# A Gram-matrix product in three passes on split parts, with one part kept in HBM between batches

## The chip, the cores and the metric

One core of a Trainium2 chip runs the whole kernel. The metric is the device time of one execution in microseconds (us). The profile and the trace come from one further execution of the same program; their times are in us from the start of its span, and durations of single instructions are in ns where it says so.

## What is computed

A decoder layer in fp32 on 8 batches of 512 tokens with 512 features. Three blocks follow each other, each with a layer norm ahead of it and a residual behind it:

1. A linear attention without softmax. The reference writes it token by token:

```python
Q = jnp.einsum('btae,aeqf->qbtaf', x, qw)
pre = jnp.einsum('qbtaf,buqf->qbtau', Q, x)
attn = jnp.einsum('qbtau,buqg->abtqg', pre, x)
out = jnp.einsum('abtk,akg->btag', attn, combiners)
```

   Since nothing nonlinear stands between the factors, the kernel first forms the Gram matrix of the normalised tokens per head q, G_q = y_q^T y_q (128 x 128), then T_q = G_q times the combiners of that q (128 x 512), then M = the queries times T, and last x + rstd * (centred x) M. "Combiner product" is the product T_q.

2. Cross attention with a context of 512 tokens per batch, softmax, biases.

3. A shared expert of 704 hidden features plus a mixture of 16 experts with top-2 routing and a capacity per expert.

## The kernel before, in words

**Three passes.** Most large products are not done as plain fp32 matmuls. Each operand is split once into an upper part (a copy into the type fp32r, made by ScalarE) and a lower part (the difference of the value and its upper part, made by VectorE or GpSimd). `three_pass` (L62 to L72, its matmuls are all on L71) then adds three matmuls per product: upper times upper, upper times lower, lower times upper. The queries, scores, values, probabilities and all expert products go that way. The Gram matrix (L785, from the `f32_group` helper), the combiner product (L886), the product M (L785 too) and A (L921) are plain fp32 matmuls. A fp32 matmul shows as two records in the trace.

**Order of the work.** The order is written out by hand in `phase2` (`order`, a list of named steps), and every engine walks the same list and does its own share of each step. Iteration i mixes the cross attention of batch i with the linear attention of batch i+1: Y1T(i), V(i), ST0(i+1), LN0(i+1), MEAN(i+1), STORE(i-1), Q(i), G(i+1), T(i+1), SC(i), M(i+1), PT(i), C(i+1), A(i+1), LN1(i+1), PV(i), LN2(i). On TensorE, step G ends with the first of four score tiles of batch i (`scores(b - 1, 0)`, 12 matmuls), then T does four fp32 matmuls of 512 columns, then SC does the other three score tiles (36 matmuls), then M. At i = 0 the step V(0) has been done earlier. Names such as INIT, WV and QB occur for batch 0 alone.

**The steps that the change touches.** ScalarE's part of G copies the bank with the Gram matrix to the tile G (row 12 of the scratch area, where a row is 2 KB of every partition), and counts `s_ev["G"]`; TensorE's part of T waits for that count (`drained(pe, "G", b)`). ScalarE's part of T copies the four results to y. In SC, VectorE takes the maximum of each score tile (L701), and ScalarE writes the exponentials to `prob`, rows 88 to 91. These rows hold the raw query weights during INIT. The combiners (CT, 1 MB) lie in rows 4 to 7 from the start (L282) and are read by T alone. Row 43 holds zeros that two DMAs of GpSimd write to HBM early on (`fill_tables`, semaphore `s_pad`); nobody reads it later in phase 1 save the tokens of the experts near the end.

**The DMA queue of SyncE.** SyncE issues its DMAs in the order of the list: in step A the transposed x of the next batch after A's last matmul (L311, L312), in MEAN the store of 512 means (L302), a wait for its landing and the load of the row of means into all partitions (L306), in STORE the batch's output and normalised tokens (L325, L328) and the x of three batches ahead, in C the context of the next batch (L291). GpSimd subtracts the row of means from the transposed x (L379), and TensorE's step A waits for that.

**Behind the batches.** After the last batch come the experts (`phase2`, L71 with 512 or 320 columns and L1432), with weights streamed by SyncE, split by ScalarE (L1246) and GpSimd (L1188).

Of the kernel before, what the change touches and what calls it, by code (L numbers as in the profile page):

```python
# [29 lines left out]
F32 = mybir.dt.float32  # L30
F32R = mybir.dt.float32r
# [43 lines left out]
def build(nc, a):  # L75
    Y = nc.dram_tensor("tokens_normed", (N + PAD, 2 * D), U16, kind="Internal").ap()

    slots = nc.dram_tensor("slots", (E * CAP, 2), F32, kind="Internal").ap()
    means = nc.dram_tensor("means", (B, S), F32, kind="Internal").ap()
    with ExitStack() as ctx:  # L80
        def sb(name, shape, dt):
            return ctx.enter_context(nc.sbuf_tensor(name, shape, dt))

        base, _ = nc.bump_sbuf(ROWS * D * 4)
        placed = []

        def at(row, shape, dt=F32):

            placed.append(row)
            return nc.alloc_sbuf_tensor_at(f"buffer{len(placed)}", [P] + shape, dt, offset=base + int(row * D * 4))  # L90

        shared = {
            "ident": sb("ident", [P, P], F32),
            "slot_list": sb("slot_list", [P, NSLOT, 2], F32),
            "slots": slots,
            "means": means,
            "ps": [ctx.enter_context(nc.psum_tensor(f"ps{i}", [P, 512], F32)) for i in range(BANKS)],
        }
        attn = phase1(nc, ctx, a, Y, shared, at)
        phase2(nc, ctx, a, Y, shared, at, attn)  # L100


def phase1(nc, ctx, a, Y, shared, at):
    out = a["out"]
    ident, slot_list, slots = shared["ident"], shared["slot_list"], shared["slots"]
    means = shared["means"]
    ps = shared["ps"]

    def sb(name, shape, dt):
# [2 lines left out]
    def sem(name):  # L112
        return ctx.enter_context(nc.semaphore(name))
# [36 lines left out]
    VWH, VWL = at(30, [NC, D], F32R), at(34, [NC, D], F32R)  # L150
    QT = at(0, [H, H, P])
    CT = at(4, [H, H * P])
    key_row, bv_all = at(50, [D]), at(51, [D])
    rw = sb("rw", [P, NC, E], F32)
    rwp = sb("rwp", [P, NC, 2 * E], F32R)
# [16 lines left out]
    xT = at(8, [NC, S])  # L172
    mean_row, zeros = at(42, [S]), at(43, [D])
    G = at(12, [H * P])
    M = at(13, [H * P])
    y1h, y1l = at(68, [NC, S], F32R), at(72, [NC, S], F32R)
    qh, ql = at(52, [NC, S], F32R), at(56, [NC, S], F32R)
# [76 lines left out]
    s_mean, s_mstored, s_mrow = sem("s_mean"), sem("s_mstored"), sem("s_mrow")  # L254
    s_xT, s_centred = sem("s_xT"), sem("s_centred")
    s_cnt = sem("s_cnt")

    def sync(sp):
        def load_x(b):
            if b >= XS:  # L260

                sp.wait_ge(s_out, 16 * (b - XS + 1))
            sp.dma_start(x[b % XS][:], a["x"][b].rearrange("(t p) d -> p t d", p=P)).then_inc(s_x[b % XS], 16)

        def small_loads():
            for dst, src in ((bias_col[:, 0:NC], a["bq"].rearrange("(c p) -> p c", p=P)),
                             (bias_col[:, NC:2 * NC], a["bk"].rearrange("(c p) -> p c", p=P)),
                             (bv_all[:], a["bv"].partition_broadcast(P)),
                             (rb_all[:], a["rb"].partition_broadcast(P)),
                             (rw[:], a["rw"].rearrange("(c p) e -> p c e", p=P))):  # L270
                with nc.allow_non_contiguous_dma(reason="a few columns of biases"):
                    sp.dma_start(dst, src).then_inc(s_small, 16)  # L272

        for j in range(NC):
            rows = slice(j * P, (j + 1) * P)
            sp.dma_start(wq_raw[:, j, :], a["WqT"][rows, :]).then_inc(s_wqk[j], 16)
            sp.dma_start(wk_raw[:, j, :], a["WkT"][rows, :]).then_inc(s_wqk[j], 16)  # L277
            if j == 1:
                load_x(0)
        small_loads()  # L280
        sp.dma_start(wv_raw[:], a["Wv"].rearrange("(c p) n -> p c n", p=P)).then_inc(s_wv, 16)
        sp.dma_start(CT[:], a["CT"]).then_inc(s_w, 16)  # L282
        sp.dma_start(QT[:], a["QT"]).then_inc(s_w, 16)

        def load_transposed(b):
            sp.dma_start(xT[:], a["xT"][b].rearrange("(c p) n -> p c n", p=P)).then_inc(s_xT, 16)

        load_transposed(0)

        def load_context(b):  # L290
            sp.dma_start(craw[:], a["ctxT"][b].rearrange("(c p) k -> p c k", p=P)).then_inc(s_c, 16)  # L291

        load_context(0)

        def step(name, b):
            if name == "C" and b >= 1:
                sp.wait_ge(s_cl, NC * b)
                load_context(b)
            if name == "MEAN":
                sp.wait_ge(s_mean, b + 1)  # L300
                with nc.allow_non_contiguous_dma(reason="one number per partition and tile"):
                    sp.dma_start(means[b].rearrange("(t p) -> p t", p=P), mean[:]).then_inc(s_mstored, 16)  # L302
                sp.wait_ge(s_mstored, 16 * (b + 1))
                if b >= 1:
                    sp.wait_ge(s_centred, NC * b)
                sp.dma_start(mean_row[:], means[b].partition_broadcast(P)).then_inc(s_mrow, 16)  # L306
                if b == 0:
                    for first in range(1, XS):
                        load_x(first)
            if name == "A" and b + 1 < B:  # L310
                filled(sp, "A", b, NT - 1)  # L311
                load_transposed(b + 1)  # L312
            if name == "TURN":
                if b == 0:
                    sp.wait_ge(s_out, 16 * (B - 1))
                    for stored in s_yout:
                        sp.wait_ge(stored, 16 * NT * (B - 1) // 2)
                for t in range(NT):
                    sp.dma_start_transpose(turned(b, t)[:], Y[b * S + t * P:b * S + (t + 1) * P, :])\
                        .then_inc(s_turn, 16)  # L320
            if name == "STORE":
                rows = slice(b * S, (b + 1) * S)
                sp.wait_ge(s_base, NT * (b + 1))
                sp.wait_ge(s_out, 16 * b)
                sp.dma_start(out[rows, :].rearrange("(t p) d -> p t d", p=P), x[b % XS][:]).then_inc(s_out, 16)  # L325
                for t in range(NT):
                    sp.wait_ge(s_halves, NT * b + t + 1)
                    sp.dma_start(Y[b * S + t * P:b * S + (t + 1) * P, :],  # L328
                                 halves(b, t)[:].rearrange("p two d -> p (two d)")).then_inc(s_yout[t % 2], 16)
                if b + XS < B:  # L330
                    load_x(b + XS)
        return step
# [97 lines left out]
    def scalar(act):  # L430
# [15 lines left out]
        def step(name, b):  # L446
# [55 lines left out]
            if name == "Q":  # L502
                for c in range(NC):
                    filled(act, "Q", b, c)
                    bank = bank_of("Q", b, c)
                    act.activation(qh[:, c, :], bank[:], ACT.Identity, bias=qbias[:, 2 * c:2 * c + 1])\
                       .then_inc(s_qh, 1)
            if name == "G":
                filled(act, "G", b)
                bank = bank_of("G", b, 0)  # L510
                copy(G[:], bank[:]).then_inc(s_ev["G"], 1)
            if name == "SC":
                for t in range(NT):
                    act.wait_ge(s_nb, NT * b + t + 1)
                    filled(act, "SC", b, t)
                    bank = bank_of("SC", b, t)
                    act.activation(prob[:, t, :], bank[:], ACT.Exp, bias=nbias[:, t:t + 1],
                                         scale=SCALE, accum_out=rsum[:, t:t + 1]).then_inc(s_ev["SC"], 1)
# [21 lines left out]
    def vector(dve):  # L540
# [68 lines left out]
        def step(name, b):  # L609
# [71 lines left out]
            if name == "Y1T":  # L681
                for c in range(NC):
                    dve.wait_ge(s_y1h, NC * b + c + 1)
                    filled(dve, "Y1T", b, c)
                    bank = bank_of("Y1T", b, c)
                    dve.tensor_tensor(y1l[:, c, :], bank[:], y1h[:, c, :].bitcast(F32), ALU.subtract)\  # L686
                        .then_inc(s_ev["Y1T"], 1)
            if name == "Q":
                for c in range(NC):
                    dve.wait_ge(s_qh, NC * b + c + 1)  # L690
# [91 lines left out]
    def tensor(pe):  # L782
# [20 lines left out]
        def step(name, b):  # L803
# [74 lines left out]
            if name == "T":  # L878
# [3 lines left out]
                    drained(pe, "W", 0, NC - 1)  # L882
                drained(pe, "Q", b - 1, 3)
                drained(pe, "G", b)
                for q in range(H):
                    pe.matmul(bank_of("T", b, q)[:], G[:, q * P:(q + 1) * P], CT[:, q, :],  # L886
                              start=True, stop=True).then_inc(s_mm["T"], 1)
            if name == "SC":
                if b == B - 1:
                    drained(pe, "V", b, 1)  # L890
# [57 lines left out]
def phase2(nc, ctx, a, Y, shared, at, attn):  # L948
# [70 lines left out]
    for i in range(-1, B):  # L1019
# [13 lines left out]
            steps.append(("V", 0))  # L1033
        if i == 0:
            steps.remove(("V", 0))
        for name, b in steps:
            if 0 <= b < (1 if name in ("INIT", "WV", "QB") else B):
                order.append((name, b))
# [448 lines left out]
```

## Time and profile before

| | |
|---|---|
| median of 3 runs | 1865.12 us (1864.83 to 1865.19) |
| the profiled execution's own time | 1865.53 us |
| its span | 1863.8 us |
| TensorE busy | 1836.5 us, 99% of the span |
| TensorE weight loads | 1616.4 us, 87% |
| VectorE, ScalarE, GpSimd busy | 834.7, 745.2, 880.4 us |

The busy time of TensorE is a union of records whose ends are modelled, so that a record can reach over the start of the next. The distance from start to start, or a piece of the chain of work, tells what a matmul costs in the stream.

### The profile page before, as it was taken

Reading aid. Unit: us, or ns where it says so; the run is one execution under the profiler, and the core shown is the slowest. Engines: PE = TensorE matmul, PEld = TensorE weight load, DVE = VectorE, ACT = ScalarE, POOL = GpSimd, SP = SyncE. Lnnn points to the kernel's source line nnn. Section 1 sums busy time; section 2 is a strip of 40 time slices with the busy share of each in tenths; the row PEclk is TensorE's granted clock in tenths of the full one; section 3 lists DMA queues with packets and bytes.
Section 4 is the critical chain, followed back from the end, with each engine's and each line's share of the span. In section 5 each row is a group of like instructions: output and inputs, shape, how many; then the busy total and the mean of one; then the engine's idle time right before and its main releaser. Section 6 shows DMA issues by size and latency. Waiting matters only on the chain.

```text
span 1863.8 us, 27056 instructions
## 1 busy us (share of the span) xinstructions
PE 1836.5 (99%) x10096; PEld 1616.4 (87%) x10096; DVE 834.7 (45%) x2015; ACT 745.2 (40%) x1468; POOL 880.4 (47%) x759
## 2 busy tenths in 40 slices
PE   7899999999999999999999999999999999999997
PEld 4788888888887887888899999999999999999996
DVE  3565567556765444343342334433444334443332
ACT  2344443444454333332444344443444434444331
POOL 2235333533563423222656665566655666556631
PEclk9899999999999999999999999999999999999999
DMA  7303212322273333321766666666666676666722
GB/s 238 108 25 119 96 63 80 120 98 73 92 180 57 47 46 74 52 46 18 160 153 153 146 142 129 156 153 148 141 130 155 156 147 142 131 152 157 143 46 29
DMA packets 218098, 209.68 MB, mean 112 GB/s; under 512 B 137424, under 2 KB 137424, under 8 KB 217712
## 3 DMA queue, kind: packets, MB, share of 16 engines
q1 hardware_dynamic: 192672, 154.85, 31.3%
q0 software_dynamic: 25296, 53.11, 16.8%
q8 instruction: 80, 1.31, 0.3%
q14 instruction: 50, 0.41, 0.1%
HBM read 129.63 MB, written 48.92 MB: 96 GB/s over the span
## 4 chain that ended last, share of the span: by engine, by line
PE 97%; POOL 1%; SPq 1%; DMA 0%; DVE 0%; ACT 0%; issue 0%; DVEq 0%; ACTq 0%; POOLq 0%
PE ps L71 65%; PE ps L1432 23%; PE ps L785 4%; PE ps L921 2%; PE ps L886 2%; PE ps L791 1%; POOL buffer L379 0%; DMA buffer<-in_wts 0%; POOL buffer L387 0%; SPq L272 0%; DMA rw<-in_rw 0%; ACT buffer L437 0%; PE ps L866 0%; POOL buffer L1188 0%; SPq L277 0%
## 5 line engine op out<-in xcount | busy, mean ns | idle before, releaser
L71 PE MATMUL ps<-buffer,buffer 128*128 128x320 f32 (+1 forms) x6816 | 1227.2, 341 | 2.1 <-DVE buffer L686 2.1
L71 PEld LDWEIGHTS ps<-buffer,buffer 128*128 128x128 f32 x6816 | 1106.0, 188 | 107.9 <-issue 3.5
L1188 POOL TENSOR_TENSOR buffer<-buffer,buffer 128x512 fp32r<-128x512 f32 x289 | 380.0, 1481 | 249.7 <-ACT buffer L1246 249.4
L1432 PE MATMUL ps<-buffer,buffer 128*128 128x512 f32 x1904 | 437.5, 390 | 0.8 <-DVE buffer L1334 0.8
L1432 PEld LDWEIGHTS ps<-buffer,buffer 128*128 128x128 f32 x1904 | 355.7, 188 | 75.1 <-POOL buffer L1188 1.4
L1246 ACT ACTIVATE buffer<-buffer 128x512 fp32r<-128x512 f32 (+1 forms) x491 | 294.1, 651 | 164.9 <-PE ps L1432 93.8
L1288 ACT ACTIVATE buffer<-ps 128x320 f32<-128x320 f32 (+1 forms) x240 | 112.5, 469 | 599.1 <-PE ps L71 585.1
L1350 DVE TENSOR_TENSOR ps<-ps,buffer 128x320 f32<-128x320 f32 (+2 forms) x198 | 100.2, 506 | 489.0 <-ACT buffer L1288 468.0
L1235 POOL DMA_INDIRECT out_tokens<-buffer,slot_list x80 | 125.9, 1574 | 185.4 <-DVE buffer L1380 177.1
L424 POOL DMA_INDIRECT slots<-pairs,slot_u x64 | 63.5, 993 | 182.2 <-DVE slot_u L772 165.1
L432 ACT ACTIVATE buffer<-ps 128x512 fp32r<-128x512 f32 (+1 forms) x148 | 81.6, 600 | 120.1 <-PE ps L71 39.9
L437 ACT ACTIVATE buffer<-buffer,shift,rstd 128x512 f32<-128x512 f32 x96 | 70.4, 805 | 135.2 <-DVE shift L579 135.2
L1380 DVE TENSOR_SCALAR buffer<-ps,slot_list 128x512 f32<-128x512 f32 x80 | 59.7, 746 | 112.2 <-PE ps L1432 112.2
L1334 DVE TENSOR_TENSOR buffer<-ps,buffer 128x320 fp32r<-128x320 f32 (+2 forms) x198 | 96.5, 488 | 11.0 <-ACT buffer L1246 10.0
L1201 POOL DMA_INDIRECT buffer<-tokens_normed,slot_list x80 | 83.5, 1044 | 28.5 <-issue 28.5
L398 POOL TENSOR_TENSOR buffer<-buffer,buffer 128x512 f32<-128x512 f32 x32 | 42.1, 1348 | 116.0 <-DVE shift L579 105.2
L1246 ACT ACTIVATE buffer<-ps 128x320 fp32r<-128x320 f32 (+2 forms) x198 | 86.3, 436 | 0.3 <-DVE ps L1350 0.3
L387 POOL TENSOR_TENSOR buffer<-buffer,buffer 128x512 fp32r<-128x512 f32 x32 | 41.1, 1320 | 91.1 <-ACT buffer L432 91.1
L1318 DVE COPY buffer<-buffer 128x512 uint16<-128x512 uint16 x80 | 72.7, 931 | 0.5
L1350 DVE TENSOR_TENSOR buffer<-ps,buffer 128x512 f32<-128x512 f32 (+1 forms) x42 | 29.0, 690 | 96.7 <-ACT buffer L1288 96.2
L563 DVE BATCH_NORM_STATS2 stats<-buffer 128x6 f32<-128x512 f32 x96 | 61.2, 682 | 0.5
L701 DVE TENSOR_REDUCE smax<-ps 128x1 f32<-128x512 f32 x32 | 22.1, 691 | 86.4 <-PE ps L71 86.4
(116 smaller groups left out, 1116.6 us busy)
## 6 DMA issues: line engine op xcount, KB each, us to landing
buffer<-in_wts SPq DMA_DIRECT2D x289, 256.0 KB
buffer<-in_x SPq DMA_DIRECT2D x8, 1024.0 KB, 6.1
buffer<-in_xT SPq DMA_DIRECT2D x8, 1024.0 KB, 5.5
buffer<-in_ctxT SPq DMA_DIRECT2D x8, 1024.0 KB, 7.9
out_tokens<-buffer SPq DMA_DIRECT2D x8, 1024.0 KB, 6.0
tokens_normed<-buffer SPq DMA_DIRECT2D x32, 256.0 KB, 3.0
out_tokens<-buffer POOLq DMA_DIRECT2D x32, 256.0 KB, 5.4
buffer<-means SPq DMA_DIRECT2D x8, 256.0 KB, 4.6
```

What stands on the lines that cost most here:

```text
L71: last = pe.matmul(out, left, right, start=(c == 0 and i == 0), stop=(c == len(parts) - 1 and i == 2))
L432: return act.activation(dst, src, ACT.Copy)
L785: last = pe.matmul(out, left, right, start=(i == 0), stop=(i == len(pairs) - 1))
L1188: pool.tensor_tensor(wl[n % RING][:], wraw[n % RAW][:], wh[n % RING][:].bitcast(F32), ALU.subtract).then_inc(s_wl, 1)
L1201: pool.indirect_dma_start(xn[:, t, :], None, Y[:, :], rows_at(groups[g][1], t), bounds_check=N + PAD - 1).then_inc(s_xg, 16)
L1235: pool.indirect_dma_start(out[:, :], rows_at(part, t), ost[:, t, :], None, bounds_check=N + PAD - 1, compute_op=ALU.add).then_inc(s_add[t] ...
L1246: return act.activation(dst, src, ACT.Copy)
L1288: act.activation(silu[u % TMP][0:rows_of(c), 0:n], bank[0:rows_of(c), 0:n], ACT.Silu)\
L1318: dve.tensor_copy(halves_of(t)[:, :, :, 0], xp[t][:, NC:2 * NC, :]).then_inc(s_xlow, 1)
L1334: dve.tensor_tensor(lo[:, first:first + n], product_of(u)[0:rows, 0:n], hh[0:rows, c, first:first + n].bitcast(F32), ALU.subtract).then_in ...
L1350: dve.tensor_tensor(product_of(u)[0:rows_of(c), 0:n], up_bank[u % 2][rows, 0:n], silu[u % TMP][0:rows_of(c), 0:n], ALU.mult).then_inc(s_ht, 1)
L1432: ins = pe.matmul(down_bank[n % 2][:], left, right, start=(c == 0 and i == 0), stop=(c == FC - 1 and i == len(passes) - 1))
```

## The change

From batch 1 on the combiner product T is done with `three_pass` on split parts; batch 0 stays a plain fp32 product. The parts of the combiners are made once, in iteration 0: a new step SPLIT has ScalarE copy CT to `ct_hi` (rows 88 to 91, type fp32r) and SyncE store that to a new tensor `combiners` in HBM (1 MB); a new step LOW has VectorE write the difference over CT itself (`ct_lo`, rows 4 to 7). As the exponentials overwrite rows 88 to 91 in every batch, SyncE loads `ct_hi` again from HBM after step A of batches 1 to 6, for T of batches 2 to 7. In G, from batch 1 on, ScalarE writes `g_hi` (row 12) and VectorE then writes `g_lo` (row 43), and VectorE's instruction now counts `s_ev["G"]`. ScalarE's step SC of batch 0 waits for the store of `ct_hi`.

```diff
+    ct_hi, ct_lo = at(88, [H, H * P], F32R), at(4, [H, H * P], F32R)
+    g_hi, g_lo = at(12, [H * P], F32R), at(43, [H * P], F32R)
...
     # SyncE
             if name == "A" and b + 1 < B:
                 filled(sp, "A", b, NT - 1)
                 load_transposed(b + 1)
+                if b >= 1:
+                    sp.dma_start(ct_hi[:].bitcast(F32), combiners).then_inc(s_ct_loaded, 16)
+            if name == "SPLIT":
+                sp.wait_ge(s_ct_hi, H)
+                sp.dma_start(combiners, ct_hi[:].bitcast(F32)).then_inc(s_ct_stored, 16)
...
     # ScalarE
+            if name == "SPLIT":
+                for q in range(H):
+                    copy(ct_hi[:, q, :], CT[:, q, :]).then_inc(s_ct_hi, 1)
             if name == "G":
                 filled(act, "G", b)
                 bank = bank_of("G", b, 0)
-                copy(G[:], bank[:]).then_inc(s_ev["G"], 1)
+                if b == 0:
+                    copy(G[:], bank[:]).then_inc(s_ev["G"], 1)
+                else:
+                    copy(g_hi[:], bank[:]).then_inc(s_g_hi, 1)
             if name == "SC":
+                if b == 0:
+                    act.wait_ge(s_ct_stored, 16)
...
     # VectorE
+            if name == "LOW":
+                for q in range(H):
+                    dve.wait_ge(s_ct_hi, q + 1)
+                    dve.tensor_tensor(ct_lo[:, q, :], CT[:, q, :], ct_hi[:, q, :].bitcast(F32), ALU.subtract)\
+                        .then_inc(s_ct_lo, 1)
+            if name == "G" and b >= 1:
+                if b == 1:
+                    dve.wait_ge(s_pad, 32)
+                dve.wait_ge(s_g_hi, b)
+                filled(dve, "G", b)
+                bank = bank_of("G", b, 0)
+                dve.tensor_tensor(g_lo[:], bank[:], g_hi[:].bitcast(F32), ALU.subtract).then_inc(s_ev["G"], 1)
...
     # TensorE, step T
                 drained(pe, "G", b)
+                if b == 1:
+                    pe.wait_ge(s_ct_lo, H)
+                if b >= 2:
+                    pe.wait_ge(s_ct_loaded, 16 * (b - 1))
                 for q in range(H):
-                    pe.matmul(bank_of("T", b, q)[:], G[:, q * P:(q + 1) * P], CT[:, q, :],
-                              start=True, stop=True).then_inc(s_mm["T"], 1)
+                    cols = slice(q * P, (q + 1) * P)
+                    if b == 0:
+                        ins = pe.matmul(bank_of("T", b, q)[:], G[:, cols], CT[:, q, :], start=True, stop=True)
+                    else:
+                        ins = three_pass(pe, bank_of("T", b, q)[:],
+                                         [(g_hi[:, cols], g_lo[:, cols], ct_hi[:, q, :], ct_lo[:, q, :])])
+                    ins.then_inc(s_mm["T"], 1)
...
     # the order, iteration 0
         if i == 0:
             steps.remove(("V", 0))
+            steps.insert(steps.index(("ST0", 1)), ("SPLIT", 0))
+            steps.insert(steps.index(("INIT", 1)), ("LOW", 0))
```

## Rows read from the trace of the kernel before

**Rows 1.** The page: the chain that ended last, by engine.
```profile
PE 97%; POOL 1%; SPq 1%; DMA 0%; DVE 0%; ACT 0%; issue 0%; DVEq 0%; ACTq 0%; POOLq 0%
```

**Rows 2.** Waits of TensorE: us in total, times, longest.
```profile
PE ps L921 <- POOL buffer L379: 8.5, 1, 8.5
...
PE ps L71 <- DVE buffer L686: 2.1, 1, 2.1
```

**Rows 3.** The chain that ended last, in order of time: start us, us, what.
```profile
90.69 3.43 PE ps L886 x8
...
149.22 2.74 PE ps L71 x12
151.96 3.43 PE ps L886 x8
155.39 8.17 PE ps L71 x36
163.56 3.57 PE ps L785 x32
...
172.45 10.90 PE ps L71 x48
```

**Rows 4.** Groups of TensorE by shape: busy us, mean ns of one; then the weight loads.
```profile
L71 PE MATMUL ps<-buffer,buffer 128*128 128x320 f32 x4224 | 622.1, 309 | 0.0
...
L71 PEld LDWEIGHTS ps<-buffer,buffer 128*128 128x128 f32 x6816 | 1106.0, 188 | 107.9 <-issue 3.5 <-DVE buffer L686 2.3 <-DVE buffer L711 0.3
```

**Rows 5.** Timeline of ScalarE, batches 0 to 2: start us, us [idle before <-releaser].
```profile
67.80 2.56 ACT L432 ACTIVATE buffer<-ps 128x512 fp32r<-128x512 f32 x5 [0.45 <-PE ps L71]
79.58 2.94 ACT L437 ACTIVATE buffer<-buffer,shift,rstd 128x512 f32<-128x512 f32 x4 [9.22 <-DVE shift L579]
...
149.26 0.60 ACT L432 ACTIVATE buffer<-ps 128x512 f32<-128x512 f32 x1 [2.82 <-PE ps L785]
```

**Rows 6.** Timeline of VectorE, same columns.
```profile
79.30 0.16 DVE L579 SCALAR_TENSOR_TENSOR shift<-mv,rstd 128x4 f32<-128x4 f32 x1
83.12 2.78 DVE L693 SCALAR_TENSOR_TENSOR buffer<-ps,qbias,buffer 128x512 fp32r<-128x512 f32 x4 [3.66 <-ACT buffer L506]
...
144.75 2.72 DVE L693 SCALAR_TENSOR_TENSOR buffer<-ps,qbias,buffer 128x512 fp32r<-128x512 f32 x4 [3.66 <-ACT buffer L506]
152.06 0.69 DVE L701 TENSOR_REDUCE smax<-ps 128x1 f32<-128x512 f32 x1 [4.59 <-PE ps L71]
```

**Rows 7.** Timeline of GpSimd, same columns.
```profile
39.70 4.61 POOL L387 TENSOR_TENSOR buffer<-buffer,buffer 128x512 fp32r<-128x512 f32 x3
...
92.14 5.00 POOL L379 TENSOR_TENSOR buffer<-buffer,buffer 128x512 f32<-128x512 f32 x4 [23.21 <-DMA buffer<-means]
...
146.21 2.29 POOL L409 COPY buffer<-buffer 128x512 uint16<-128x512 uint16 x4
```

**Rows 8.** Groups by shape: copies and differences of the split, mean ns of one.
```profile
L432 ACT ACTIVATE buffer<-buffer 128x512 fp32r<-128x512 f32 x68 | 37.3, 636 | 0.0
...
L663 DVE TENSOR_TENSOR buffer<-ps,buffer 128x512 fp32r<-128x512 f32 x32 | 21.4, 678 | 7.1 <-ACT buffer L432 6.7
L634 DVE TENSOR_TENSOR buffer<-buffer,buffer 128x512 fp32r<-128x512 f32 x32 | 20.0, 686 | 9.0 <-ACT buffer L432 9.0
...
L623 DVE TENSOR_TENSOR buffer<-buffer,buffer 128x512 fp32r<-128x512 f32 x4 | 5.8, 1514 | 8.4 <-ACT buffer L432 8.4
```

**Rows 9.** Timeline of SyncE's DMA issues: start us, us.
```profile
77.06 0.37 SPq L302 DMA_DIRECT2D means<-mean  x1
...
111.22 0.37 SPq L286 DMA_DIRECT2D buffer<-in_xT  x1
```

**Rows 10.** DMA issues: count, KB each, median us to landing.
```profile
out_tokens<-buffer SPq DMA_DIRECT2D x8, 1024.0 KB, 6.0
...
buffer<-in_CT SPq DMA_DIRECT2D x1, 1024.0 KB, 8.5
...
means<-mean SPq DMA_DIRECT2D x8, 2.0 KB, 10.1
```

More of the change, by code:

```diff
@@ L79, in build @@
     means = nc.dram_tensor("means", (B, S), F32, kind="Internal").ap()
+    combiners = nc.dram_tensor("combiners_top", (P, H * H * P), F32, kind="Internal").ap()
     with ExitStack() as ctx:
@@ L96, in build @@
             "means": means,
+            "combiners": combiners,
             "ps": [ctx.enter_context(nc.psum_tensor(f"ps{i}", [P, 512], F32)) for i in range(BANKS)],
@@ L106, in phase1 @@
     means = shared["means"]
+    combiners = shared["combiners"].rearrange("p (h n) -> p h n", h=H)
     ps = shared["ps"]
@@ L256, in phase1 @@
     s_cnt = sem("s_cnt")
+    s_ct_hi, s_ct_lo, s_ct_stored, s_ct_loaded = (sem(f"s_ct_{k}") for k in ("hi", "lo", "stored", "loaded"))
+    s_g_hi = sem("s_g_hi")
     def sync(sp):
```

## The prediction
> **What bounds the kernel now.** I began with the chain of waits that ended last: 97% of it is TensorE [rows 1], so the span is TensorE's own work in order. The list of TensorE's waits says the same from the other side: the two longest that lie behind the first 50 us are 8.5 us and 2.1 us, each once, before batch 1 has even begun its Gram matrix [rows 2]. From there to the experts I followed the chain in order of time [rows 3]. It repeats with a period of 151.96 - 90.69 = 61.27 us per batch, and its pieces touch: 149.22 + 2.74 = 151.96, 151.96 + 3.43 = 155.39, 155.39 + 8.17 = 163.56. So in the part that the change touches, a microsecond taken off TensorE comes off the end, as long as no other engine becomes late by it, and the questions are two: what the new product costs on TensorE, and whether its operands come in time.
>
> **The product itself.** Before, T is four fp32 matmuls in 3.43 us (8 records, 429 ns each) [rows 3]. After, it is 4 x 3 = 12 passes of 512 columns. The price of a pass stands in the same chain: the 48 passes of PV take 10.90 us, 227 ns each; the 36 of the scores 8.17 us, also 227 ns; the 12 ahead of T 2.74 us, 228 ns, a little more since they follow a fp32 product [rows 3]. Twelve passes cost 12 x 0.227 = 2.72 us, so a batch saves 3.43 - 2.72 = 0.71 us. Seven batches (1 to 7) take that way: 7 x 0.71 = 5.0 us. For the pass price I take 227 ns, because T's new neighbours on both sides are passes of the same kind. The upper end is 233 ns (2.74 us over 12 passes plus a handoff from fp32 as long again, 0.06 us): saving 0.63 us a batch, 4.4 us in all. The lower end is 227 ns with the dearer handoff between T and the scores gone as well, some 0.02 us a batch: 5.1 us.
>
> Here a rule speaks against the change, since it adds weight loads: 12 per batch where there were 8. In the rows a load takes 188 ns, yet the passes with 320 columns follow each other every 622.1 / 4224 = 0.147 us, less than one load [rows 4]; the loads run beside each other and beside the matmuls, and what sets the distance is the columns. Twelve loads x 188 ns = 2.26 us also lie below the 2.72 us of their passes. The Trainium skill (Perfetto Trace Analysis, section Identifying the Most-Contended Engine) says that the busy share of the weight loads, not that of the matmuls, tells how near TensorE is to its limit; by it, T would grow from 8 loads to 12. The trace does not agree that loads are the limit here; I keep it as a rival below.
>
> **The Gram matrix in two parts.** ScalarE's copy stays one instruction of 0.60 us; in batch 2 it runs from 149.26 to 149.86 [rows 5]. New is VectorE's difference behind it, from a bank and a tile: 678 ns by the same shape in the step Y1T [rows 8]. With a handoff of 0.10 us (an estimate: the score tile ends at 151.96 and its maximum starts at 152.06 [rows 3, 6]) it ends at 149.86 + 0.10 + 0.68 = 150.64. TensorE is in the first score tile until 151.96 [rows 3], and T may start then: 1.3 us to spare. VectorE is free for it: the four differences of Q end at 144.75 + 2.72 = 147.47, and its next work is the maximum at 152.06 [rows 6], which waits for the score tile anyway. Nothing is queued behind it that could be late. Its cost on the path is zero; if the cover (the score tile, 2.74 us) were gone, it would be 0.78 us a batch. The period repeats to a hundredth of a microsecond, so one batch stands for seven.
>
> **Splitting the combiners, once.** On ScalarE four copies of 636 ns [rows 8] go in after its evictions of Y1T, which end at 70.36, in a gap of 9.22 us before 79.58 [rows 5]: done at about 72.9, hidden; without the gap 2.5 us, once. On VectorE four differences go in behind ST0, after 79.30 + 0.16 = 79.46, ahead of a wait of 3.66 us for the first Q tile, which ends at 83.12 [rows 6]. At 686 ns each [rows 8] they take 2.7 us and end at 82.2: hidden. Their upper bound is 1514 ns each, what such a difference took while GpSimd was at work [rows 7, 8]: 6.1 us, end 85.5. Then the four differences of Q come 2.4 us late and end at 88.3, and the score tile, due at 149.22 - 61.27 = 87.95, would wait about 0.5 us, once [rows 3]. GpSimd has nothing to do there before 92.14 [rows 7], so I take the lower. T of batch 1 needs these parts at 90.69; 8 us to spare.
>
> **SyncE's queue.** The store of the upper part is issued at about 73, once, ahead of the means at 77.06 [rows 9]. No other DMA is then in the way of its 6.0 us (the output's store of the same size) [rows 10], so it lands near 79 to 80, and the exponentials that wait for it come after T(1), which starts at 90.69. The store of the means (10.1 us to landing) and the row of means can be pushed back by at most those 6.0 us; GpSimd's subtraction then ends at 92.14 + 5.00 + 6.0 = 103.1 instead of 97.1 [rows 7]. A(1) comes behind M, which in batch 1 ends at 163.56 + 3.57 - 61.27 = 105.9 today [rows 3]. Still hidden, with 2 us left once T is shorter. The six loads go out directly after the transposed x (111.22) [rows 9]; even with 8.5 us for each megabyte, one behind the other [rows 10], they are there by 129, and T(2) wants them at 151.96. SyncE waits for nothing new in step A, and what it issues next, the store of the means, is due a period after 77.06, at 138.3. Zero, with over 20 us to spare.
>
> **The new wait of TensorE** (one more semaphore in T) is met long before T by the times above. Two stand there today, and the chain shows no idle time at them; I take zero, with 0.05 us a batch, 0.35 us in all, as the upper end (an estimate: no more than the 0.06 us of a handoff above). Of what follows T, ScalarE copies four banks of 0.60 us each, now filled every 0.68 us in place of 0.86 us: it keeps up, and M comes 8.17 us later. Everything later in the period hangs on TensorE by fixed lags that do not contain T.
>
> **Sum.** -5.0 (product) + 0 + 0 + 0 = -5.0 us. Against the profiled execution's 1865.53 us that is 1860.5 us; its own time lies 0.4 us over the median of the runs, 1865.12 us, so the median after is 1860.1 us.
>
> **The rivals.**
>
> *Part of it is given back* (0.14). Some engine that was just in time becomes the end of a wait, or the experts' part, where DMA and GpSimd are busier, takes some of the 5 us again. For it: the kernel has been packed so tight that a single lag of 1.3 us covers the difference above. Against: the lags are cut by nothing, since T lies in none of them, and TensorE waits for nearly nothing today. It gives anything between 1860.8 and 1865.1 us; a fifth of it I count as still faster by over 0.2%.
>
> *T waits for the lower part of the Gram matrix* (0.04), the case on the slower side. Place: the difference on VectorE between ScalarE's copy and T. It costs nothing up to 1.3 us of lateness, cancels the saving at 1.3 + 0.71 = 2.0 us, and makes the kernel slower from there. The one thing that could hold VectorE so long is GpSimd: its copies of 2.29 us end at 148.5 [rows 7], 1.4 us ahead. If they moved back over the difference and held it for their full length, and the difference ran anew behind them, it would end at 150.64 + 2.29 + 0.68 = 153.61, 1.65 us late: 7 x (1.65 - 0.71) = 6.6 us slower, 1871.7 us. Against it: the difference reads one operand from PSUM, and its like (678 ns mean over 32) shows no such stretching, while the one with both operands in SBUF does [rows 8]. The Trainium skill (SBUF — State Buffer, section Who interferes with whom) names two SBUF inputs as what makes a VectorE instruction contend with GpSimd; the rows agree, 1514 against 678 ns.
>
> *Passes priced as fp32 records or by their weight loads* (0.02). If each of the twelve took the 429 ns of a record of T, on the ground that loads set the pace or that these tiles are not run as the other passes are, T would cost 5.15 us: +1.72 x 7 = 12.0 us, 1877.1 us. The 227 ns of every other stretch of passes is against it.
>
> **How the numbers follow.** The forecast has 0.80: 1860.1 us, by itself 1859.9 to 1860.8 with the pass price's ends and the new waits. A change of 0.2%, 3.73 us (about what a measurement of this kernel can tell from no change), ends at 1861.39 us, so the forecast's whole range is on the faster side. Faster by over 0.2%: 0.80 + 0.03 = 0.83. Within 0.2%: 0.11. Slower: 0.04 + 0.02 = 0.06. The range goes from 1859.4 us (another 0.5 us for runs on another day) to 1861.8 us, which takes in the nearer part of the first rival; the rest of the cases that it leaves out have less than 2 in 10.
>
> **What would show it.** In the profile after: T as 12 passes of 227 ns, 2.72 us in the chain; a period of 60.55 us; T starting right behind the score tile in each batch, with no idle time of TensorE put down to the new difference; VectorE's difference done about 1.3 us earlier; and the start of the experts 5.0 us earlier, kept to the end. Wrong would be: a period over 60.9 us, a wait of TensorE in T or A(1), or an end that comes less early than the experts' start.

## The result and the profile after

The changed kernel is faster. Over 15 runs each, the median is 1860.16 us against 1863.99 us for the kernel before on the same chips, and the ratio of the two is 0.9978 with a 95% interval of 0.9970 to 0.9987. The profiled execution took 1860.16 us, with a span of 1858.4 us against 1863.8 us.

The page of the changed kernel begins with the busy time of the engines and has the chain's shares by engine further down.

```profile
PE 1831.5 (99%) x10124; PEld 1621.4 (87%) x10124; DVE 843.5 (45%) x2026; ACT 747.1 (40%) x1472; POOL 880.5 (47%) x759
...
PE 92%; issue 4%; SPq 1%; DMA 1%; POOL 1%; DVE 0%; ACT 0%; POOLq 0%; DVEq 0%
```

TensorE has 5.0 us less work (1836.5 - 1831.5) in 28 more records: seven batches lose 8 fp32 records and gain 12 passes. Its weight loads have grown by 5.0 us, and VectorE's time by 8.8 us. Neither shows in the span. The share of "issue" in the chain (time in which nothing that the profile shows was waited for) is new, but no wait of TensorE stands behind it: 59.39 us of it are one piece that begins at 814.37 us, among the experts, where the chain runs through other engines, and from 814 to 874 us TensorE is busy for 60.00 us of the 60. TensorE's own list of waits (us in total, times, longest) begins with the same three as before; two of them are in [rows 2].

```profile
PE ps L963 <- POOL buffer L392: 8.5, 1, 8.5
PE ps L841 <- DMA buffer<-in_WkT: 4.3, 1, 4.3
PE ps L71 <- DVE buffer L707: 2.1, 1, 2.1
...
PE ps L1476 <- DVE buffer L1378: 0.6, 1, 0.6
PE ps L1476 <- POOL buffer L1232: 0.3, 1, 0.3
```

The last two lie near 906 us; in the kernel before, the same place has one wait of 0.8 us.

The chain of waits of the changed kernel in order of time (start us, us, what) answers to [rows 3]:

```profile
84.11 3.57 PE ps L818 x32
87.68 13.62 PE ps L71 x60
101.29 3.57 PE ps L818 x32
...
144.64 3.57 PE ps L818 x32
148.21 13.62 PE ps L71 x60
161.83 3.57 PE ps L818 x32
```

The first score tile, T and the other three score tiles are now one piece of 60 passes, 13.62 us, 227 ns each. Before, it was 2.74 + 3.43 + 8.17 = 14.34 us [rows 3]. The difference is 0.72 us; the period is 148.21 - 87.68 = 60.53 us in place of 61.26 to 61.27.

The operands come as forecast. First ScalarE, then VectorE around the split and the first lower part of the Gram matrix (timelines of the changed kernel; start us, us, idle before and what ended it):

```profile
69.92 2.22 ACT L445 ACTIVATE buffer<-buffer 128x512 fp32r<-128x512 f32 x4
79.29 2.94 ACT L450 ACTIVATE buffer<-buffer,shift,rstd 128x512 f32<-128x512 f32 x4 [7.15 <-DVE shift L600]
...
87.71 0.60 ACT L445 ACTIVATE buffer<-ps 128x512 fp32r<-128x512 f32 x1 [2.88 <-PE ps L818]
```

```profile
79.09 2.49 DVE L712 TENSOR_TENSOR buffer<-buffer,buffer 128x512 fp32r<-128x512 f32 x4
82.83 2.78 DVE L726 SCALAR_TENSOR_TENSOR buffer<-ps,qbias,buffer 128x512 fp32r<-128x512 f32 x4 [1.25 <-ACT buffer L519]
88.40 0.69 DVE L720 TENSOR_TENSOR buffer<-ps,buffer 128x512 fp32r<-128x512 f32 x1 [2.78 <-ACT buffer L445]
90.52 0.69 DVE L734 TENSOR_REDUCE smax<-ps 128x1 f32<-128x512 f32 x1 [1.43 <-PE ps L71]
```

L720 is the new difference. It ends at 89.09, and T may start at 87.68 + 12 x 0.228 = 90.42: 1.3 us to spare. The four differences of the combiners (L712) lie in VectorE's idle time ahead of the Q tiles and leave 1.25 us of it.

SyncE's issues (timeline), and the landings of the new transfers (count, KB each, median us to landing):

```profile
72.17 0.34 SPq L325 DMA_DIRECT2D combiners_top<-buffer  x1
76.78 0.37 SPq L309 DMA_DIRECT2D means<-mean  x1
87.06 0.33 SPq L313 DMA_DIRECT2D buffer<-means  x1
...
110.63 0.51 SPq L322 DMA_DIRECT2D buffer<-combiners_top  x1
```

```profile
buffer<-combiners_top SPq DMA_DIRECT2D x6, 1024.0 KB, 7.4
...
combiners_top<-buffer SPq DMA_DIRECT2D x1, 1024.0 KB, 3.9
```

The store has landed at 76.1, before the means are issued, so it pushes nothing back. The load lands near 118, 33 us ahead of its T.

### The profile page after: what moved, and what is told of

The parts are those of the page before. It is cut to its first block, busy times and chain, and to the rows that moved or that the text cites. A ratio compares the mean times of both kernels' runs of the same rounds, so it can differ in the third digit from the quotient of the medians.

```text
span 1858.4 us, 27141 instructions
## 1 busy us (share of the span) xinstructions
PE 1831.5 (99%) x10124; PEld 1621.4 (87%) x10124; DVE 843.5 (45%) x2026; ACT 747.1 (40%) x1472; POOL 880.5 (47%) x759
## 4 chain that ended last, share of the span: by engine, by line
PE 92%; issue 4%; SPq 1%; DMA 1%; POOL 1%; DVE 0%; ACT 0%; POOLq 0%; DVEq 0%
PE ps L71 63%; PE ps L1476 21%; PE ps L818 4%; PE ps L963 2%; PE ps L824 1%; DMA slot_list<-slots 0%; SPq L1176 0%; POOL buffer L392 0%; PE ps L925 0%; POOL buffer L400 0%; SPq L332 0%; DMA rw<-in_rw 0%; SPq L279 0%; POOL buffer L1232 0%; DMA buffer<-tokens_normed,slot_list 0%
## 5 line engine op out<-in xcount | busy, mean ns | idle before, releaser
L71 PE MATMUL ps<-buffer,buffer 128*128 128x320 f32 (+1 forms) x6900 | 1242.1, 341 | 2.1 <-DVE buffer L707 2.1
L71 PEld LDWEIGHTS ps<-buffer,buffer 128*128 128x128 f32 x6900 | 1121.7, 188 | 108.2 <-DVE buffer L707 2.3
L1476 PEld LDWEIGHTS ps<-buffer,buffer 128*128 128x128 f32 x1904 | 355.8, 188 | 75.3 <-POOL buffer L1232 1.7
L422 POOL COPY buffer<-buffer 128x512 uint16<-128x512 uint16 x64 | 37.1, 620 | 50.2 <-DMA tokens_normed<-buffer 50.2
```

Of the source, the lines that this page charges most:

```text
L71: last = pe.matmul(out, left, right, start=(c == 0 and i == 0), stop=(c == len(parts) - 1 and i == 2))
L1476: ins = pe.matmul(down_bank[n % 2][:], left, right, start=(c == 0 and i == 0), stop=(c == FC - 1 and i == len(passes) - 1))
```

## The experiments

The theory is: the gain is the product's alone, TensorE's time comes off the end one to one, and all the new work is hidden, the new difference with 1.3 us of slack. The rivals are that the new work costs something, that other engines take the time back, and the two slower cases of the prediction. Each edit is against the changed kernel.

**Only the product undone.**

```diff
-ins = three_pass(pe, bank_of("T", b, q)[:], [(g_hi[:, cols], g_lo[:, cols], ct_hi[:, q, :], ct_lo[:, q, :])])
+ins = pe.matmul(bank_of("T", b, q)[:], g_hi[:, cols].bitcast(F32), ct_hi[:, q, :].bitcast(F32), start=True, stop=True)
```

> Everything of the change is kept (the split of the combiners, the lower part of the Gram matrix and its place in the counting, the store and the six loads), only the product from batch 1 on is again one plain fp32 matmul per head, on the upper parts; the lower parts are made and not used. Theory (all of the gain is the product's, the rest is hidden): a period of 61.27 us as before, the time of the kernel before within 0.3 us, so a ratio of 1.000 to it. Rival (the rest costs something that the product has to pay for first): slower than before, by 0.1 us a batch or more, 0.7 us in all upwards. Rival (the new order of the split itself helps): faster than before.

The ratio to the kernel before is 1.0005 (0.9995 to 1.0015; median 1866.81 us over 12 runs, against 1865.61 us over 24). Its chain, in order of time:

```profile
142.93 3.57 PE ps L818 x32
146.50 2.74 PE ps L71 x12
149.24 3.43 PE ps L927 x8
152.67 8.17 PE ps L71 x36
160.84 3.57 PE ps L818 x32
```

Piece by piece this is [rows 3]. The period, from A to A, is 61.26 us in every batch. So in the batches everything of the change but the passes costs and brings nothing: of the first rival's 0.1 us a batch the period leaves nothing. The times say less: the expectation's 0.3 us is finer than they can tell, and the interval leaves up to 0.15% slower and 0.05% faster.

**No reload.**

```diff
-                if b >= 1:
-                    sp.dma_start(ct_hi[:].bitcast(F32), combiners).then_inc(s_ct_loaded, 16)
...
-                if b >= 2:
-                    pe.wait_ge(s_ct_loaded, 16 * (b - 1))
...
+                        top = ct_hi if b == 1 else WH
```

> The six loads of the upper part and TensorE's wait for them are left out; from batch 2 on the product takes another resident upper part of the same shape, so its values are not the product's. Theory (the loads are hidden): the period of the changed kernel, 60.54 us, and its span of 1858.4 us within 0.3 us. Rival (a megabyte more per batch slows something down): a shorter period, 60.4 us or less, 1857.5 us or less.

The period is 60.53 us, as with the loads. The span was 1857.3 us, 1.1 us less, which alone would speak for the rival; but 0.4 us of it lie ahead of A(1) (106.05 against 106.45), and the rest in one place among the experts near 906 us, over 400 us after the last load, where TensorE waited 0.64 and 0.26 us in the changed kernel and 0.17 us here. The loads do not make that wait: the run with the product undone has all six and waits 0.16 us there, and the kernel before has none and waits 0.76 us. The ratio to the kernel before is 0.9971 (0.9960 to 0.9983; median 1859.16 us over 6 runs), which holds the changed kernel's. In the batches, by the period, the loads are hidden.

**Two passes.**

```diff
+for i, (left, right) in enumerate([(g_hi[:, cols], ct_hi[:, q, :]), (g_hi[:, cols], ct_lo[:, q, :])]):
+    ins = pe.matmul(bank_of("T", b, q)[:], left, right, start=(i == 0), stop=(i == 1))
```

> The third pass (lower part of the Gram matrix times upper part of the combiners) is left out, 4 matmuls a batch less; the sum lacks that term. Theory (TensorE's own time comes off the end one to one, 227 ns a pass): 0.91 us a batch, 6.4 us in all: period 59.63 us, span 1852.1 us against 1858.4. Rival (another engine takes the time back as TensorE gets shorter): less than 5 us of it, with a wait of TensorE in the period.

```profile
147.47 2.73 PE ps L71 x12
150.20 1.81 PE ps L928 x8
152.02 8.16 PE ps L71 x36
```

Eight passes take 1.81 us, 227 ns each (the chain again). The period is 59.63 us, 0.90 us less for four passes less, with no wait in it: in the batches TensorE's time comes off one to one here too. The span is 1852.5 us, 5.9 us less, where the expectation had 6.4. A(1), the step A of batch 1, starts only 0.75 us earlier (105.70 against 106.45) though one period's saving of 0.90 lies ahead of it, and the wait near 900 us has grown from 0.64 to 0.90 us. So a small part is lost outside the batches, where the expectation put nothing; ahead of A(1) it can be the clock at the start, of which more below. The ratio to the kernel before is 0.9944 (0.9932 to 0.9957). It is faster than both kernels, but it is another computation: the term of the Gram matrix's lower part is gone. I do not count it as a better version of this one.

**The changed kernel again**, on the chip of these three:

> The changed kernel once more beside the others, to have its own spread on the same chip. By the traces so far its span is 5.4 us under the one before: 5.1 us in seven periods (7 x 0.73), 0.3 us ahead of them. If that is what the change is worth, the medians differ by 5.1 us here too (1857.6 us where the one before has 1862.7 us); the 3.8 us between the medians of 15 runs would be an accident of how many executions had the lower clock at the start. If it is worth less, the difference stays near 3.8 us.

Median 1861.11 us over 11 runs against 1865.61 us: 4.5 us, ratio 0.9980 (0.9971 to 0.9989). The period is 60.53 us again. This stands between the two numbers of the expectation and settles little by itself. Against the run with the product undone, on this same chip (1866.81 us), it is 5.7 us. The traces say more. Its span was 1857.0 us, 1.4 us less than that of the first profile, and A(1) started 1.57 us earlier (104.88 against 106.45): all of it, and a little more, lies in the first 105 us. The windows of TensorE show where (us, busy us, granted clock as a share of 2.4 GHz, DMA share, GB/s), in the first profile of the changed kernel and then in this one:

```profile
72.00:74.00 2.00, 2.00 (x8) 0.63 0.55 229
74.00:76.00 2.00, 2.00 (x7) 0.52 0.73 295
```

```profile
72.00:74.00 2.00, 2.00 (x10) 1.00 0.62 262
74.00:76.00 2.00, 2.00 (x11) 1.00 0.65 262
```

It is one kernel with the same work. In one execution the granted clock is at its lower level (1.2 GHz in place of 2.4) for most of these 4 us, just behind TensorE's wait of 2.1 us from 69 to 71 us; in the other it stays at the upper level. Both executions also have the lower level around TensorE's idle 8.5 us at A(0), from 46 us to beyond 54. How long that stretch lasts differs as well. In 10 us steps, the kernel before and then the run with the product undone:

```profile
50.00:60.00 10.00, 9.74 (x47) 0.72 0.87 269
...
70.00:80.00 10.00, 8.43 (x30) 0.83 0.03 0
```

```profile
50.00:60.00 10.00, 9.80 (x52) 0.84 0.85 271
...
70.00:80.00 10.00, 9.60 (x42) 1.00 0.28 105
```

Both do the same work on TensorE, and A(1) started at 107.46 in the one and at 104.74 in the other. Among the five profiles in which T took the 13.62 us piece of the changed kernel, A(1) started between 104.88 and 109.32 us, but from there to the end of the span it was 1751.2 to 1752.1 us in all of them. The times of the changed kernel spread over 6.3 us (1857.08 to 1863.42 us), more than the change is worth, and so 15 runs still leave an interval of 1.7 parts in a thousand. Here too the clock goes with the time: the six runs below 1859 us have a mean granted clock of 0.995, the six above 1861 us have 0.992 or 0.993.

**The difference later, by one and by four repeats.**

```diff
+                for _ in range(4):
+                    link(dve.tensor_tensor(g_lo[:], bank[:], g_hi[:].bitcast(F32), ALU.subtract))
                 dve.tensor_tensor(g_lo[:], bank[:], g_hi[:].bitcast(F32), ALU.subtract).then_inc(s_ev["G"], 1)
```

> VectorE makes the lower part of the Gram matrix twice, one behind the other with a wait between, before it counts it: T's operand comes about 0.72 us later. In the changed kernel it is ready about 1.3 us before T may start. Theory (slack of 1.3 us): the period stays 60.53 us. Rival (the slack is smaller than the rows show, and part of it is already used): a longer period, up to 61.2 us.

> The same five times over: the operand comes about 2.9 us later. Theory (slack of 1.3 us, beyond it every microsecond is TensorE's): TensorE waits 1.6 us in each of seven batches before T, a period of 62.1 us, 11 us over the changed kernel and about 6 us over the one before. Rival (VectorE's lateness is absorbed by later slack of TensorE): the period stays under 61 us.

With one repeat the period is 60.53 us in every batch: no cost there (one run, 1862.80 us). With four it is 62.41 to 62.44 us, the median 1872.02 us (5 runs) and the ratio to the kernel before 1.0035 (1.0020 to 1.0049). The profiled execution was the slowest of the five, 1879.40 us; the other four took 1870.98 to 1872.20 us. VectorE's timeline with four repeats, and the chain:

```profile
153.50 2.87 DVE L721 TENSOR_TENSOR buffer<-ps,buffer 128x512 fp32r<-128x512 f32 x4 [2.40 <-ACT buffer L445]
156.40 0.69 DVE L722 TENSOR_TENSOR buffer<-ps,buffer 128x512 fp32r<-128x512 f32 x1
```

```profile
152.83 2.73 PE ps L71 x12
155.57 1.62 issue
157.19 11.16 PE ps L71 x48
```

The counted difference starts 2.90 us late, and TensorE stands for 1.62 us, so the slack was 2.90 - 1.62 = 1.28 us. The 48 passes after the wait take 11.16 us where they otherwise take 10.90 [rows 3]: starting anew costs another 0.26 us. The granted clock does not explain it, since it is 1.00 from 152 to 169 us. Together 1.88 us, which is the 1.9 us by which the period has grown. Nothing in the period takes it back.

**No cover.** The score tile behind T instead of ahead of it:

```diff
-                if b >= 1:
-                    drained(pe, "Q", b - 1, NC - 1)
-                    scores(b - 1, 0)
             if name == "T":
...
                     ins.then_inc(s_mm["T"], 1)
+                if b >= 1:
+                    drained(pe, "Q", b - 1, NC - 1)
+                    scores(b - 1, 0)
```

> The first score tile (12 matmuls) is issued behind T instead of ahead of it, nothing else. Theory (the chain bank to ScalarE's copy to VectorE's difference to T is hidden by that tile alone): from the end of the Gram matrix to the end of the difference it is 1.4 us in the changed kernel, so TensorE waits about 1.45 us per batch ahead of T, a period of 62.0 us, 10.2 us over the changed kernel, about 5 us over the one before. Rival (TensorE's queue or the weight loads hide part of it, or the maxima of the scores come late in their turn): below 1.2 us or above 1.8 us per batch.

```profile
149.22 3.57 PE ps L818 x32
152.79 1.46 issue
154.25 13.88 PE ps L71 x60
```

The wait is 1.46 us (the chain of this kernel), and the restart adds 0.26 us (13.88 against 13.62): 1.72 us, period 62.24 to 62.26 us. The median is 1872.82 us (5 runs), the ratio to the kernel before 1.0045 (1.0030 to 1.0060). The same three passes that gain 5 us would then lose about 7 us against the kernel before, by the periods (7 x 0.99 us), and 5.6 to 11.2 us by the interval. The wait was expected to a hundredth; the restart was not.

**M in passes of 128 columns**, on stand-ins for its operands.

```diff
+                    if b == 0:
                         last = f32_group(bank_of("M", b)[:, cols], [(QT[:, h, q, :], y[:, q, cols]) for q in range(H)])
+                    else:
+                        last = three_pass(pe, bank_of("M", b)[:, cols],
+                                          [(WH[:, q, cols], WL[:, q, cols], VWH[:, q, cols], VWL[:, q, cols])
+                                           for q in range(H)])
```

> The product M, too, in three passes from batch 1 on, 48 matmuls of 128 columns in place of 16 fp32 ones (32 records, 3.57 us), on resident split tiles that stand in for its operands, so its values are not M's. It asks what a pass of few columns costs. If the columns set the distance as between 512 columns (227 ns) and 320 columns (147 ns), that is 0.417 ns a column plus 14 ns, a pass costs 67 ns: 3.2 us, 0.35 us a batch less, period 60.2 us. If a weight load sets the least distance (the fp32 records of 128 columns follow each other every 112 ns with a load each), a pass costs about 110 ns: 5.3 us, 1.7 us a batch more, period 62.3 us.

```profile
148.99 3.57 PE ps L818 x32
152.56 18.93 PE ps L71 x108
```

Of the 18.93 us, 60 passes of 512 columns take 13.62, so the 48 passes of 128 columns take 5.31 us: 111 ns each, against 3.57 us for M in plain fp32. The period is 62.28 us and the ratio to the kernel before 1.0039 (1.0025 to 1.0053). The line through 512 and 320 columns, which would have given 67 ns, does not hold down there. The fp32 records of 128 columns have the same spacing, 3.57 / 32 = 112 ns. That a weight load is what sets it fits the count of loads, one each, but the run does not separate it from any other cost per matmul, so the cause of this floor is not shown.

**T in passes of 256 columns.**

```diff
+for half in (slice(0, 256), slice(256, 512)):
+    ins = three_pass(pe, bank_of("T", b, q)[:, half], [(g_hi[:, cols], g_lo[:, cols], ct_hi[:, q, half], ct_lo[:, q, half])])
```

> T in passes of 256 columns, 24 a batch in place of 12 of 512. A pass took 227 ns at 512 columns, 147 ns at 320 and, in the run with M in passes, 110 ns at 128. If the distance is 0.417 ns a column plus 14 ns down to a floor of 110 ns, a pass of 256 columns takes 121 ns: T 2.90 us, 0.18 us a batch more, period 60.71 us. If the floor lay higher than the run with 128 columns shows (a weight load of 188 ns seen whole), 4.5 us and a period of 62.3 us.

```profile
148.45 13.80 PE ps L71 x72
162.25 3.57 PE ps L818 x32
```

The 24 passes take 13.80 - 48 x 0.227 = 2.90 us, 121 ns each, and the period is 60.71 us, both as expected. At 256 columns the line still holds. The one run took 1862.28 us, with a span of 1860.6 us, 2.2 us over the changed kernel's where seven batches account for 1.3; near 908 us TensorE waits 2.1 us in all, against 0.9 us. That wait among the experts was between 0.2 and 2.6 us in the profiles here, in no order that follows the change.

**GpSimd at work beside the difference.**

```diff
...
                 for t in range(NT):
+                    if t == 2 and b <= B - 3:
+                        pool.wait_ge(s_g_hi, b + 2)
+                        for _ in range(6):
+                            link(pool.tensor_tensor(idle_out[:], idle_in[:], idle_in[:], ALU.add))
                     n = NT * b + t
```

> GpSimd is given six additions of 128 x 256, both inputs in SBUF, on tiles of their own, started by the same count as VectorE's difference for the Gram matrix of batches 2 to 7, between its second and third copy of the token halves; the results are used by nobody. It tests the slower rival: a difference with one operand in PSUM held up by GpSimd. Theory (not held up, as its mean of 678 ns had it): the difference keeps its 0.69 us and the period stays 60.53 us. Rival (held for GpSimd's length): the difference ends 1.3 to 4 us later, TensorE waits ahead of T, and the period goes over 61 us.

GpSimd's and VectorE's timelines of that run:

```profile
148.98 4.07 POOL L422 TENSOR_TENSOR idle_out<-idle_in 128x256 f32<-128x256 f32 x6 [1.44 <-ACT buffer L451]
```

```profile
148.94 0.69 DVE L726 TENSOR_TENSOR buffer<-ps,buffer 128x512 fp32r<-128x512 f32 x1 [2.40 <-ACT buffer L451]
```

The two run at the same time, the difference keeps its 0.69 us, and the period its 60.53 us. But GpSimd began 0.04 to 0.05 us after the difference in every batch, so the run does not show a GpSimd that is at work first, which is what the rival had. The changed kernel's own profile does:

```profile
63.65 5.05 POOL L428 TENSOR_TENSOR buffer<-buffer,buffer 128x512 f32<-128x512 f32 x4 [9.94 <-ACT buffer L450]
```

```profile
66.19 2.65 DVE L684 TENSOR_TENSOR buffer<-ps,buffer 128x512 fp32r<-128x512 f32 x4 [3.55 <-ACT buffer L445]
```

These four differences of the same shape start while GpSimd is at work, and none of the 32 on that line takes more than 693 ns. The ratio to the kernel before on that chip is 0.9949 (0.9930 to 0.9969, 4 runs against 5). That is more than the change is worth by the period; the runs are few, and all five of the kernel before had a granted clock of 0.993, the other four 0.993 to 0.996.

## Why the prediction was right

**The price of the product** was the step that carries the sum, and it came out as put: 12 passes of 227 ns, with the handoff between fp32 and passes saved, 0.72 to 0.73 us a batch where the sum had 0.71. The run with the product undone gives back the old period, and the one with two passes moves it by 0.90 us for 0.91 expected.

**One to one with the end.** The trace has 7 x 0.73 = 5.1 us in the batches and 0.3 us ahead of them, together the 5.4 us between the two spans. A piece of 68 passes in the experts' part starts at 564.30 us in place of 569.67, 5.4 us earlier; behind the waits near 906 us the lead is 5.2 us (907.60 against 912.77), and at the end 5.4 us again. From A(1) to the end of the span the kernel before took 1756.3 us and the run with the product undone 1755.3 us, against 1751.2 to 1752.1 us in five profiles with the product in passes: 3.1 to 5.1 us, where six periods make 6 x 0.73 = 4.4 us. Between the medians it is 3.8 us (15 runs each) and 4.5 us on another chip (11 against 24), where the sum said 5.0. The intervals of both ratios hold 5.0 us (a ratio of 0.9973), and the spread ahead of A(1) is larger than the gap. The first rival, that part is given back, has only tenths of a microsecond in the traces for it, in the wait near 906 us; that the whole 5.1 us arrive in the medians is argued from the traces and not measured to better than the intervals. The predicted 1860.1 us is near the measured 1860.16 partly by luck: the sum started from 1865.12 us, 1.1 us over what 15 runs of the kernel before gave. From their 1863.99 us the same sum ends at 1859.0 us, below the stated range.

**The difference behind ScalarE's copy** was given 1.3 us of slack. One repeat was free, four showed 1.28 us. The slower rival had its place and its slack right, and the runs without cover and with four repeats show what lies beyond: more than the wait, since the prediction priced a wait at its length and left out the 0.26 us of the restart. So the saving would be used up at about 1.28 + 0.73 - 0.26 = 1.75 us of lateness (an estimate from the two runs), and not at 2.0. The prediction's 0.78 us a batch without the cover was the difference's part alone: the run without cover has 1.46 us of wait, since ScalarE's copy of 0.60 us is then uncovered too. The rival's cause, GpSimd, does not hold for a difference with one operand in PSUM, neither when GpSimd begins after it nor when it is at work first; its own case, the uint16 copies over the new difference, occurred in no run.

**The split and the queue** were hidden as put. LOW took 2.49 us for 2.7 forecast; the store landed in 3.9 us for 6.0, so that the pushing back of the means, up to 6 us in the prediction, did not happen at all.

**The rule on weight loads.** The Trainium skill (Perfetto Trace Analysis, section Identifying the Most-Contended Engine) has the busy share of the loads, beside the share of peak matmul rate, as the measure of how near TensorE is to its limit, in place of the matmuls' busy share. The prediction's rival made of it that more loads cost time. For passes of 512 columns they do not: the loads' busy time grew by 5.0 us here while the kernel became faster. This does not speak against the page, which gives a measure of nearness and no price of a load. At 128 columns something of a fixed size per matmul sets the pace (111 ns), and there three passes cost more than fp32 (5.31 against 3.57 us). The dismissal in the prediction, from the 147 ns at 320 columns, was right for T and would have been wrong for M.

## What to carry to other kernels

Where a trace shows TensorE without gaps, a product's fp32 records and the spacing of passes of the same width in their own rows are enough to price a change to three passes; at 512 columns it gave 0.72 us on 3.43 us, at 128 columns it cost 1.74 us on 3.57 us, in the run with M. The extra step between bank and matmul must lie under other work of TensorE: look for what is issued between, compare its length with the new chain, and count a wait as its length plus the restart (0.26 us in the two runs here). When one kernel's runs spread more than the change is worth, compare the period of a repeated stretch in the traces, which here repeats to a hundredth of a microsecond wherever TensorE does not wait in it.

## What was not expected of the hardware

- A pass has a floor: 227 ns at 512 columns, 147 ns at 320, 121 ns at 256, and 111 ns at 128, where the line through the others would give 67 ns.
- After a wait of 1.46 or 1.62 us, the 60 or 48 passes that follow take 0.26 us more in all than in a stream, with the granted clock at 1.00.
- The granted clock in the first 80 us differs between executions of the same kernel: two profiles of the changed one reached A(1) at 106.45 and at 104.88 us. In five profiles A(1) spread over 4.4 us and the rest of the execution over 0.9 us. That the 6.3 us over which its 15 runs spread lie there too fits their granted clocks (0.992 to 0.995), but only the profiled ones show the place.
